# A decoder layer on one core: x of batches 1 to 3 is loaded with its features on partitions, and its sums stand elsewhere in GpSimd's queue

## The reference

```python
xn = layernorm(x)                                    # x: 4 x 512 x 1024, over the 1024 features
q, k, v = xn @ Wq.T, xn @ Wk.T, xn @ Wv.T            # 32 query heads, 8 key/value heads, 128 each
q, k = rmsnorm(q) * q_norm_w, rmsnorm(k) * k_norm_w
p = softmax(q @ k.T / sqrt(128) + alibi, causal)
s = (p @ v) @ Wo.T
g = silu(xn @ W.T + bias + lora(xn))
out = x + s * g
```

## Time and profile before

| | |
|---|---|
| median of 3 runs | 2655.3 us (2654.3 to 2657.4) |
| profiled execution | 2655.7 us, its span 2653.9 us |
| matrix products and transposes | 13840 |
| busy: TensorE, VectorE, ScalarE, GpSimd | 97%, 64%, 66%, 65% |
| DMA traffic | 414.8 MB, 156 GB/s |

### The profile page before, as it was taken

One profiled execution on the slowest core, in us unless ns is written; L12 is line 12 of the kernel. 1 busy time (PEld: TensorE's weight loads), 2 busy tenths in 40 slices (PEclk: granted clock), 3 DMA queues, 4 the chain that ended last, 5 costly groups with the idle time before them and its releaser, 6 DMA issues.

```text
span 2653.9 us, 39893 instructions
## 1 busy us (share of the span) xinstructions
PE 2583.1 (97%) x13840; PEld 2288.9 (86%) x13840; DVE 1699.8 (64%) x3533; ACT 1764.6 (66%) x4633; POOL 1718.0 (65%) x839
## 2 busy tenths in 40 slices
PE   6789999999999999999999999999999999999997
PEld 5778888888888888888888888888888888888886
DVE  7565656666766665666667666666666756656656
ACT  4565666767767666667766667666777666667764
POOL 3577887785767565655667756565666766656555
PEclk9899999999999999999999999999999999999999
DMA  7868878875354333433344433433334533333323
GB/s 283 289 219 278 265 261 272 271 258 166 118 171 154 113 106 118 140 112 118 106 137 155 128 119 111 144 106 118 109 104 137 189 106 108 115 116 112 112 78 131
DMA packets 171896, 414.78 MB, mean 156 GB/s; under 512 B 31024, under 2 KB 63920, under 8 KB 170800
## 3 DMA queue, kind: packets, MB, share of 16 engines
q1 hardware_dynamic: 170144, 410.19, 47.1%
q10 hardware_dynamic: 1552, 2.04, 0.2%
HBM read 339.81 MB, written 89.13 MB: 162 GB/s over the span
## 4 chain that ended last, share of the span: by engine, by line
PE 90%; DVE 3%; DMA 2%; POOL 2%; ACT 1%; SPq 1%; issue 0%; ACTq 0%; POOLq 0%; DVEq 0%
PE proj L508 21%; PE proj L510 21%; PE proj L509 21%; PE tr L608 5%; PE tr L588 3%; PE sc L508 3%; PE sc L509 3%; PE sc L510 3%; PE ot L509 3%; PE ot L510 3%; PE ot L508 3%; DMA wu<-xtok 1%; PE tr L581 1%; DMA wl<-wu 1%; POOL wl L1081 1%
## 5 line engine op out<-in xcount | busy, mean ns | idle before, releaser
L1081 POOL TENSOR_TENSOR wl<-wl,wh 128x896 fp32r<-128x896 f32 x428 | 909.1, 2156 | 552.3 <-ACT wh L788 552.2
L508 PE MATMUL proj<-wh,xh 128*128 128x448 f32 x1792 | 670.7, 374 | 7.3 <-ACT raw L827 2.2
L509 PE MATMUL proj<-wl,xh 128*128 128x448 f32 x1792 | 657.9, 367 | 0.0
L510 PE MATMUL proj<-wh,xl 128*128 128x448 f32 x1792 | 657.8, 367 | 0.0
L1092 POOL TENSOR_TENSOR wb_lo<-wb_lo,wb_hi 128x1024 fp32r<-128x1024 f32 x128 | 307.7, 2404 | 303.7 <-ACT wb_hi L822 303.7
L879 ACT ACTIVATE misc<-misc,negmax 128x128 f32<-128x128 f32 (+3 forms) x512 | 286.7, 565 | 266.3 <-DVE negmax L1319 266.1
L508 PE MATMUL proj<-o_hi,wb_hi 128*128 128x512 f32 x1024 | 425.2, 415 | 7.4 <-DVE acc L1344 3.5
L1344 DVE TENSOR_TENSOR acc<-acc,proj 128x512 f32<-128x512 f32 x476 | 324.8, 683 | 149.7 <-PE proj L510 147.8
L858 ACT ACTIVATE pT_hi<-tr 128x512 fp32r<-128x512 f32 (+3 forms) x512 | 197.5, 440 | 325.9 <-PE tr L608 325.9
L510 PE MATMUL proj<-o_hi,wb_lo 128*128 128x512 f32 x1024 | 403.6, 394 | 0.0
L509 PE MATMUL proj<-o_lo,wb_hi 128*128 128x512 f32 x1024 | 401.3, 392 | 0.0
(11 more groups left out here) (135 smaller groups left out, 4438.1 us busy)
## 6 DMA issues: line engine op xcount, KB each, us to landing
wl<-wu SPq DMA_DIRECT2D x426, 448.0 KB, 3.9
wb_lo<-wo_in SPq DMA_DIRECT2D x128, 512.0 KB, 3.3
wu<-xtok SPq DMA_DIRECT2D x13, 1792.0 KB, 9.7
wo_in<-wo SPq DMA_DIRECT2D x32, 512.0 KB, 6.2
xtok<-wa SPq DMA_DIRECT2D x52, 256.0 KB, 4.0
wu<-xtok SPq DMA_DIRECT2D x13, 896.0 KB, 6.2
gate_dram<-misc SPq DMA_DIRECT2D x32, 256.0 KB, 5.0
xtok<-xT SPq DMA_DIRECT2D x28, 256.0 KB, 5.1
```

The costliest lines, as they stand in the source:

```text
L508: pe.matmul(out, hi_l, hi_r, start=first, stop=False, skip_group_check=onto)
L509: pe.matmul(out, hi_l, lo_r, start=False, stop=False, skip_group_check=onto)
L510: return pe.matmul(out, lo_l, hi_r, start=False, stop=last, skip_group_check=onto)
L1081: pool.tensor_tensor(w_slot(wl, w), w_slot(wl, w, True), w_slot(wh, w), ALU.subtract).then_inc(w_ready, 1)
```

## The change

Everything concerns batches 1 to 3; batch 0 is prepared as before.

- x is loaded from the array with features on partitions, so nothing is turned: per batch the 14 turns (56 transposes), their copies and subtractions from PSUM go. In their place ScalarE copies seven blocks of 128 x 1024 within SBUF (`x_hi_later`) and VectorE subtracts seven times within SBUF (`x_lo_later`).
- The statistics are taken from a second load of x with tokens on partitions, one tile of 128 tokens at a time into `rows` (steps 4.3, 5.0, 5.1, 5.2). The Newton steps stand in 5.3 in all batches. `spread_rows` writes rinv and shift out over 128 columns for each tile, TensorE turns both in step 6.0 (`turn_tokens`, eight transposes), and VectorE copies them back (`take_rows`). They now lie along the free dimension, on all partitions.
- x is normalised by four multiplications on VectorE (`x_mul`, step 6.1) and four additions on GpSimd (`x_add`, two at the end of step 6.1, two at the end of 6.3), instead of four scalings on ScalarE.
- GpSimd's P7 sum comes at the end of step 6.3, behind the low parts of P1 and P2 and the last two additions. P6's stands ahead of `low_b` in 7.0, P5's and P3's ahead of `low_b` in 7.1.
- To make room, the bias has one buffer: `bias_of(m + 1)` waits for all four maxima of step m. The scratch tile of the squares is smaller, with a semaphore step for each square.

```diff
+    at = {(6, 3): (P1, P2), (7, 0): (P7, P4, None, P6), (7, 1): (None, P5, P3)}
+    return [(b + 1, p) if p is not None else None for p in at.get((g, j), ())]
+def x_tile(n, j):
+    b, g = divmod(n, HKV)
+    t = {(4, 3): 0, (5, 0): 1, (5, 1): 2, (5, 2): 3}.get((g, j))
...
-                sp.dma_start(xtok[:], x_tok[b - 1]).then_inc(x_in, 16)
+                chunks = xT[b * NK:b * NK + NK].rearrange("k p n -> p k n")
+                sp.dma_start(flat(xtok).rearrange("p (k n) -> p k n", k=NK), chunks).then_inc(x_in, 16)
+            def load_rows(b, t):
+                if t > 0:
+                    sp.wait_ge(row_stat, NT * (b - 1) + t)
+                elif b > 1:
+                    sp.wait_ge(x_norm, 4 * (b - 1))
+                sp.dma_start(rows, x_tok[b - 1][:, t, :]).then_inc(rows_in, 16)
...
+            def x_hi_later(b, p):
+                if p in FILL_SUM:
+                    act.wait_ge(sum_ready, 4 * b + FILL_SUM[p])
+                else:
+                    act.wait_ge(x_norm, 4 * (b - 1) + {P1: 1, P2: 2, P4: 4}[p])
+                act.wait_ge(u_done, u_count(HKV * b - 1, p, 1))
+                act.activation(xh[:, p], x_block(p), ACT.Copy).then_inc(x_hi_done, 1)
...
-                if m >= 2:
-                    wait_alone(pool, scored, 4 * m - 4)
-                pool.tensor_scalar(bias_sb[:, m % 2, :], rel_sb[:], slope[:, m % H:m % H + 1], None,
+                if m >= 1:
+                    wait_alone(pool, scored, 4 * m)
+                pool.tensor_scalar(bias_sb[:], rel_sb[:], slope[:, m % H:m % H + 1], None,
...
+            def x_add(b, i):
+                part, at = x_part(i)
+                pool.wait_ge(x_mul_done, 4 * (b - 1) + i + 1)
+                pool.wait_ge(row_free, 2 * b)
+                shift = rows[:, S + at.start:S + at.stop].unsqueeze(1).to_broadcast([P, 4, 256])
+                pool.tensor_tensor(part, part, shift, ALU.add).then_inc(x_norm, 1)
...
                 bias_of(m + 1)
...
-                low_b(v + 1)
-                if (g, j) == (6, 3) and next_x is not None and b > 0:
-                    x_sum(next_x, P7)
                 if (g, j) == (7, 0) and next_x is not None:
                     x_sum(next_x, P6)
+                if (g, j) == (7, 1) and next_x is not None:
+                    x_sum(next_x, P5)
+                    x_sum(next_x, P3)
+                low_b(v + 1)
...
                     low_product(*[(n + 1, P6), (n + 1, P4), (n + 1, P3), (n + 2, P1)][j])
-                if (g, j) == (6, 3) and b == 0:
-                    x_sum(1, P7)
                 if m > 0 and j != 2:
                     low_product(*[(n + 1, P7), (n + 1, P5), None, (n + 2, P2)][j])
+                if (g, j) == (6, 1) and next_x is not None:
+                    x_add(next_x, 0)
+                    x_add(next_x, 1)
+                if (g, j) == (6, 3) and next_x is not None:
+                    x_add(next_x, 2)
+                    x_add(next_x, 3)
+                    x_sum(next_x, P7)
...
+            def spread_rows(b):
+                dve.wait_ge(ln_newton, 5 * (b + 1))
+                for i, column in enumerate((rinv_x, shift_x)):
+                    place = rows[:, i * S:i * S + S].rearrange("p (t n) -> p t n", t=NT)
+                    ins = dve.tensor_copy(place, column[:].unsqueeze(2).to_broadcast([P, NT, P]))
+                ins.then_inc(row_spread, 1)
+            def x_mul(b, i):
+                part, at = x_part(i)
+                dve.wait_ge(x_in, 16 * b)
+                dve.wait_ge(row_free, 2 * b - 1)
+                factor = rows[:, at].unsqueeze(1).to_broadcast([P, 4, 256])
+                dve.tensor_tensor(part, part, factor, ALU.mult).then_inc(x_mul_done, 1)
+            def x_lo_later(b, p):
+                dve.wait_ge(x_hi_done, x_count(b, p))
+                dve.tensor_tensor(xl[:, p], x_block(p), xh[:, p], ALU.subtract).then_inc(x_ready, 1)
...
+                if x_tile(n, j):
+                    row_stats(*x_tile(n, j))
                 if turned:
-                    x_lo(turned.pop(0))
+                    x_lo_later(*turned.pop(0))
                 add_out(v, 0)
...
-                if j == 2 and g == ln_group(b + 1) and next_x:
+                if (g, j) == (5, 3) and next_x:
                     ln_factors(b + 1)
+                    spread_rows(b + 1)
                 add_out(v, 1)
```

More of the change, by code:

```diff
@@ L93, in turn_order @@
                 keys += [("k", n + 1), ("q", n + 1, 0)]
-            keys += x_fills(n, j) + [("p", 4 * n + j, k) for k in range(NT)]
+            if (n % HKV, j) == (6, 0) and n + HKV < NG:
+                keys += [("r", n // HKV + 1, i) for i in range(2)]
+            keys += [("p", 4 * n + j, k) for k in range(NT)]
     return keys
@@ L588, in turn_rows, with turn_tokens @@
                     mm = pe.transpose(bank[:, t * P:t * P + P], raw[:, t, col:col + P], ident_sb[:])
+                mm.then_inc(tr_done, 1)
+            def turn_tokens(b, i):
+                key = ("r", b, i)
+                pe.wait_ge(row_spread, b)
+                bank = turn_bank(key)
+                for t in range(NT):
+                    at = i * S + t * P
+                    mm = pe.transpose(bank[:, t * P:t * P + P], rows[:, at:at + P], ident_sb[:])
                 mm.then_inc(tr_done, 1)
@@ L720, in step @@
                     turn_queries(n + 1, 0)
-                pieces, fills = unit_pieces(n, j), x_fills(n, j)
-                for u in pieces:
+                for i, u in enumerate(unit_pieces(n, j)):
                     piece(*u)
-                    if fills:
-                        turn_x(fills.pop(0))
+                    if (n % HKV, j) == (6, 0) and n + HKV < NG and i < 2:
+                        turn_tokens(n // HKV + 1, i)
                 if n + 1 == NG and v % 2 == 0:
@@ L828, in take_piece, with squares @@
                                proj_ps[PJ["u", n, P1, t] % 2][:, 0:HALF], ACT.Copy).then_inc(u_act, 1)
-            def squares(heads, row, turn):
-                need(act, sq_done, turn - 1)
+            def squares(heads, row, count):
                 for i, head in enumerate(heads):
                     at = (("q0", "q1", "k", "q2", "q3").index(head)) * 4 + row
-                    ins = act.activation(junk[:, turn % 2, i, :], raw[:, row, COL[head]:COL[head] + HD],
-                                         ACT.Square, accum_out=ss[:, at:at + 1])
-                ins.then_inc(sq_done, 1)
+                    need(act, sq_done, count + i - 1)
+                    act.activation(junk[:, (count + i) % 2, :], raw[:, row, COL[head]:COL[head] + HD],
+                                   ACT.Square, accum_out=ss[:, at:at + 1]).then_inc(sq_done, 1)
             def square_rows(n, p, t):
@@ L1244, in ln_stats, with row_stats, ln_variance @@
                 ins.then_inc(ln_stat, 1)
-                wait_alone(dve, ln_stat, 2 * b + 1)
+                wait_alone(dve, ln_stat, 1)
+                ln_variance(0)
+            def row_stats(b, t):
+                dve.wait_ge(rows_in, 16 * (NT * (b - 1) + t + 1))
+                for i in range(2):
+                    ins = dve.bn_stats(bn[:, t, 6 * i:6 * i + 6], rows[:, 512 * i:512 * i + 512])
+                ins.then_inc(row_stat, 1)
+                if t == NT - 1:
+                    wait_alone(dve, row_stat, NT * b)
+                    ln_variance(b)
+            def ln_variance(b):
                 for t in range(NT):
@@ L1422, in _ @@
             dve.memset(eps_x[:], LN_EPS)
-            ln_stats(0, range(3))
+            ln_stats(range(3))
             dve.wait_ge(lora_in[1], 16)
@@ L1427, in _ @@
                               ).then_inc(lora_scaled, 1)
-            ln_stats(0, range(3, NT))
+            ln_stats(range(3, NT))
             ln_factors(0)
```

150 lines of the change are left out of this document (80 added, 70 removed).

## The result

The changed kernel takes 2686.9 us (median of 4 runs, 2682.9 to 2688.1) against 2655.2 us of the kernel before (4 runs): the ratio is 1.0116, 95% interval 1.0098 to 1.0133. It is slower by 1.2%, with 144 transposes fewer on TensorE (13696 instructions against 13840).

The account below looks back on a forecast made before the run. TensorE, busy 97%, was taken to bound the kernel. Batch 0's +13.6 us and +5.8 each for batches 1 and 2 summed to +25.2 on 2655.7: 2681 us, bounds 2660.6 to 2692 (65%), overall range 2650 to 2698.

Parts of the forecast that it names:

- What can be won: Steps that turn x, over plain steps: removing the turns can give back at most 23 us, 0.9% of the time.
- Step 7.0: P7's sum late in GpSimd's queue delays ScalarE, TensorE and x's low halves: +3.3 us per batch, steps near 28 us.
- Step 0.5.3: Batch 0: Newton's lines wait for GpSimd's sums and low parts: +8.9 us once, step near 30 us.
- The clock: Half clock behind the stall in 0.5.3: +1.7 us; behind 7.0's stall nothing, VectorE being late anyway.
- 6.0, 6.1, 6.2, 6.3, 7.1: Smaller terms per batch: two turns +0.9, multiplications 0, x_add waits +1.1, turns gone less waits -0.4, and 0.
- 5.3: Batches 1 and 2, GpSimd idle: five Newton lines and two copies, less room: +0.9 us.
- row loads: Four of 512 KB behind L315, read 10 us or more later: nothing, a few us once if late.
- 0.5.2: Batch 0: last row's statistics, where Newton wasn't before: +0.7 us.
- (a): Rival: the gain arrives, P7's sum and port waits disturbing nothing: 2636 us, all below 2650; 15%.
- (b): Rival: about even, Newton meeting no sum, 7.0 at its low end, P7's sum sooner: 2658 us; 8%.
- (c): Rival: slower still, each multiplication of x meeting a GpSimd instruction and VectorE bounding 6.1, 7.0, 7.1: 2696 us; 12%.
- The total: Whole kernel: +25.2 us on the profiled 2655.7, giving 2681 us.

Follow-up runs that it names:

- The first experiment: Changed kernel with x_add 2, x_add 3 and P7's sum right behind low_b in 6.3, not behind the low parts of P1 and P2: 2670.9 us, ratio 1.0064.
- the fourth: Changed kernel with ScalarE's copies of x of P7 and P4 one piece later in 7.0, GpSimd left alone: 2684.6 us, ratio 1.0111.
- third: Changed kernel with low_b ahead of x's sums on GpSimd in 7.0 and 7.1, as in the kernel before: 2695.8 us, ratio 1.0157.
- fifth: Changed kernel with load_rows behind store_halves in steps 4.3, not ahead of it: 2686.5 us in a single execution.
- the eighth: Changed kernel with early and spread additions, Newton at 5.3's last score, row load behind the store, gate_product of 7.1 ahead of add_out 0: 2663.0 us, ratio 1.0031.

## Why the prediction was right, point by point

- **What can be won.** 23 us were said to be all that the turns cost; without any work on x the kernel takes 25.7 us less. Right, a little low: steps 5.2 and 6.2, which the 23 left out, had 1.9 us of x's work between them.
- **Step 7.0.** Predicted near 28 from the order of GpSimd's queue; 28.2 in all batches of the profiled execution. The first experiment shows that the place of P7's sum is the cause (28.2 to about 23), the fourth that the chain ends the step, not TensorE's first wait, which the prediction had said of the clock ("VectorE being late anyway"). The additions had no row; taken at 2.40, measured 2.37 each. TensorE's wait was 4.3 (4.2 predicted). One link was the other way round: the low half of P4 was to wait for P6's sum, but it went first (1336.31 to 1337.54) and the sum waited for it, 3.49 instead of 2.40, so that it ended at +20.8, not +19.2. `low_b` then followed without the low half of P4 in between, and the low half of P6 ended at +24.4 (+24.0 predicted): either order of the same pieces ends nearly alike.
- **Step 0.5.3.** Predicted near 30, measured 29.9, with two errors that cancel, which is luck. The third Newton line, one input and one output in SBUF, was taken at 0.2 and waited 1.96 like the others; the second slipped through in 0.16, in a gap of 0.1 us between two sums of GpSimd's. Where the lines meet the sums a little differently another one slips: in the first and fourth experiments, which leave them where they are, it was the third, and the first of the two copies waited instead (2.26); 0.5.3 took 31.2 and 30.9. The Trainium skill (GPSIMD Engine Reference, 1. Specifications) names both kinds as in contention, two SBUF inputs or a 2-port perf mode; I had quoted it and applied only the first half. By these rows the trace agrees with the second half also. The two elements a cycle that were left open fit the copies as well: 512 elements took 0.41 to 0.43 us (0.42 taken), where a pass of 512 that reads PSUM takes 0.68.
- **The clock.** About as large as taken (+1.7), but it can't be read from one execution. Stretches of the changed kernel (as the earlier trace rows; behind 0.5.3's stall, in steps 7.0 of the three batches, and at full clock ahead of 1.7.0):

```profile
583.90:594.10 10.20, 5.97 (x18) 5.11 (x19) 7.09 (x15) 3.05 (x7) 6.32 (x4) 0.50 0.22 63
689.70:696.50 6.80, 5.27 (x14) 4.66 (x15) 5.46 (x4) 5.22 (x8) 6.29 (x3) 0.50 0.22 64
1334.80:1338.20 3.40, 2.82 (x8) 2.52 (x9) 3.12 (x3) 3.40 (x7) 2.88 (x2) 0.50 0.00 0
1979.90:1986.70 6.80, 5.13 (x14) 4.53 (x15) 5.62 (x4) 5.10 (x8) 6.28 (x4) 0.50 0.21 62
1312.00:1319.00 7.00, 7.00 (x36) 5.55 (x37) 5.13 (x9) 5.09 (x17) 1.24 (x1) 1.00 0.53 157
```

For 10.2 us the clock was 1.2 GHz, 6 of them with TensorE at work. Part of that lies in 0.6.0, which took 23.45, 1.4 over the 22.06 of the other batches. In four experiments that leave this stall as it is (the first, third, fourth and fifth), 0.6.0 took only 21.9 to 22.3, and 0.5.3 29.5 to 31.2. The two steps together grew by 10.9 us in the changed kernel and by 9.3 to 10.8 in those four; the prediction had 8.9 + 1.7 + 0.9 = 11.5. In steps 7.0 the clock was 1.2 GHz for 6.8, 3.4 and 6.8 us, and all three took 28.2: there it cost nothing, as predicted.
- **6.0, 6.1, 6.2, 6.3, 7.1.** +0.9, 0, +1.0, -0.3 and -0.1 in batch 1 against +0.9, 0, +1.1, -0.4 and 0. 7.0 grew by 3.6 there (3.3 predicted), 5.3 by 0.5 (0.9 predicted).
- **Not foreseen.** 7.2 is 1.0 to 2.0 longer, the largest term that was missing: `gate_product` took 2.6 us behind a low part and held up VectorE's maxima of the next scores; moved, it left 7.2 at 15.3 in every batch. 0.5.0 is 1.15 longer: the row load stood ahead of a store that GpSimd's sums wait for; I had costed row loads at nothing by looking at their own readers and not at the stores queued behind them. 0.5.2 is 1.3 longer, 0.7 predicted.
- **Rivals.** (a) needed the place of P7's sum and the port waits not to matter; they did. (b) needed Newton to meet no sum and 7.0 at its low end; neither held. (c) needed each multiplication of x to meet something. In all three batches three of four took 1.2 us and one, behind `low_b`, 2.8, as the prediction's own term for 6.1 had it.
- **The total.** The median, 2686.9, lies 6 over the forecast of 2681. The groups that were summed grew by 4.0 more than predicted, about as much as the 3.9 of the three steps 7.2; the shorter start hides 2.9 of that, which is luck, and 0.8 comes from the plain steps. The last 4 are the profiled execution being the fastest one; where the slower ones spend them no profile shows.

## What to carry to other kernels

When work on SBUF alone is moved from TensorE, PSUM or ScalarE to VectorE and GpSimd, lay it out as on one shared resource: give each VectorE instruction of the kinds below a stretch in which GpSimd runs no tensor-tensor instruction, if need be with an explicit wait. In this kernel the placing decided: the same operations took 2687 us and 2646, and the change lost or won by it. Before an instruction is put behind others in a queue, look who reads its result first, and for every load what is queued behind it.

## What the runs showed of the hardware

- The exclusion works both ways. GpSimd's 1024-element additions took 3.4 us on average instead of 2.4 when VectorE's low halves ran beside them (first experiment), and a VectorE low half 2.0 to 3.5 instead of 1.2. There the two streams took turns, one instruction each.
- Which VectorE instructions wait was to be seen: those with two SBUF inputs, TENSOR_SCALAR from SBUF to SBUF (0.42 alone in the fourth experiment, 2.6 when it met `low_b` in the eighth; even with 4 elements, 1.96), and copies within SBUF (0.42 alone, 2.26 behind a low part). Those with a PSUM input kept their times (0.61, 0.69), and so did the row statistics (0.64 to 0.67 for 512 elements).
- Beside GpSimd's TENSOR_SCALAR (the bias, 1.57 us) such VectorE instructions took 0.3 to 0.5 us longer at most and didn't wait for its end.
- The half clock outlasts the wait that brought it: in 1.7.0 the product behind a wait of 4.3 us took 0.74 us, where a first product behind a short wait takes 0.44 to 0.50, and behind 0.5.3 the clock was still 1.2 GHz 3 us into the next step.
